# Two attention layers with routed experts on one core: expert outputs added to gathered rows and scattered into the result, with the stages placed anew

## The reference, cut to what matters

```python
# x: 16 batches of 512 tokens, 128 features
h = layernorm(x)
x1 = x + cosformer(h) + dense_experts(h)  # 16 heads of 8; 2 shared experts, 16 routed, top 4
h = layernorm(x1)
p = softmax(h @ router_w + router_b)      # 8 experts
e = argmax(p)                             # each token goes to one
a, g = split(h @ w1[e])                   # w1: 128 x 1024
y = (silu(a) * g) @ w2[e]                 # w2: 512 x 128
out = x1 + causal_attention(h) + max(p) * y
```

## Time and profile before

| what | value |
|---|---|
| runs shown | 1370.4, 1368.79, 1371.34 us; median 1370.4 us |
| profiled execution | 1372.72 us, of which the span from first to last instruction is 1371.5 us |
| PE busy | 1209.3 us, 88% |
| DVE busy | 991.5 us, 72% |
| ACT busy | 912.8 us, 67% |
| POOL busy | 692.6 us, 50% |
| mean granted clock of PE | 0.959 |

### The profile page before, as it was taken

The page is one execution under the profiler, slowest core; times in us unless marked ns, Lnnn a source line. Parts: engine busy times, 40 slices in busy tenths (PEclk is TensorE's granted clock), DMA queues, the critical chain, the costliest instruction groups (busy, mean ns, idle before and its releaser), DMA issues.

```text
span 1371.5 us, 28942 instructions
## 1 busy us (share of the span) xinstructions
PE 1209.3 (88%) x10216; PEld 700.1 (51%) x10216; DVE 991.5 (72%) x2378; ACT 912.8 (67%) x1233; POOL 692.6 (50%) x1093
## 2 busy tenths in 40 slices
PE   2675999999999999999999999999986999899990
PEld 1342445445454545454454545454432476799990
DVE  2163888888888988888888989888868462344545
ACT  1141777778687868777786877787773667577760
POOL 6324455554536464554545464655543345466760
PEclk9898999999999999999999999999996799999995
DMA  7323505050524416060515335060615210111118
GB/s 224 63 57 64 111 19 115 20 103 27 96 53 71 91 32 120 11 115 20 103 34 88 72 52 105 19 120 14 111 37 171 74 29 25 31 48 50 50 48 250
DMA packets 80300, 100.90 MB, mean 74 GB/s; under 512 B 8800, under 2 KB 56672, under 8 KB 79776
## 3 DMA queue, kind: packets, MB, share of 16 engines
q1 hardware_dynamic: 75680, 89.85, 29.9%
q0 software_dynamic: 4480, 9.22, 2.3%
HBM read 73.50 MB, written 25.01 MB: 72 GB/s over the span
## 4 chain that ended last, share of the span: by engine, by line
PE 63%; DVE 20%; issue 5%; ACT 4%; POOL 4%; DMA 3%; ACTq 0%; SPq 0%; DVEq 0%; POOLq 0%
PE PS L628 9%; PE PS L595 8%; PE PS L440 7%; PE PS L484 7%; PE PS L561 5%; PE PS L639 4%; PE PS L580 4%; PE PS L423 4%; DVE xn L824 3%; PE PS L434 2%; DVE nm L985 2%; DMA early<-gate_rows 2%; PE PS L462 2%; PE PS L570 2%; DVE ra L933 1%
## 5 line engine op out<-in xcount | busy, mean ns | idle before, releaser
L735 ACT ACTIVATE flow<-PS 128x1024 f32<-128x1024 f32 x320 | 321.2, 1028 | 129.4 <-PE PS L580 112.1
L1146 POOL TENSOR_SCALAR_AFFINE_SELECT flow<-flow 128x256 f32<-128x256 f32 (+1 forms) x448 | 191.0, 444 | 374.3 <-ACT flow L735 371.7
L595 PE MATMUL PS<-flow 128*32 128x512 f32 (+3 forms) x2048 | 181.2, 455 | 6.2 <-POOL flow L1146 6.2
L985 DVE TENSOR_REDUCE nm<-PS 128x2 f32<-128x1024 f32 x128 | 154.6, 1220 | 42.3 <-PE PS L549 38.9
L1133 POOL TENSOR_TENSOR early<-early 128x512 f32<-128x512 f32 x128 | 160.7, 1270 | 20.9 <-DMA early<-gate_rows 20.0
L484 PE MATMUL PS<-early,down 128*128 128x512 f32 x288 | 151.8, 637 | 18.4 <-POOL early L1133 17.9
L726 ACT COPY qp<-PS 2x1024 f16<-2x1024 f16 x128 | 128.5, 1004 | 51.0 <-PE PS L570 49.8
L440 PE MATMUL PS<-xnT,up 128*128 128x512 f32 x288 | 152.6, 625 | 3.7 <-DVE at L908 3.4
L987 DVE TENSOR_REDUCE nm<-PS 128x2 f32<-128x768 f32 x128 | 121.6, 950 | 32.4 <-PE PS L549 32.3
L628 PE MATMUL PS<-xsT,w1s 128*128 128x128 f32 x1152 | 141.5, 276 | 3.0 <-DVE act L1079 2.9
L1076 DVE SCALAR_TENSOR_TENSOR tanh<-tanh,PS 128x512 f32<-128x512 f32 x72 | 49.5, 687 | 130.0 <-ACT tanh L769 130.0
(11 more groups left out here) (178 smaller groups left out, 2263.3 us busy)
## 6 DMA issues: line engine op xcount, KB each, us to landing
early<-gate_rows SPq DMA_DIRECT2D x32, 1024.0 KB, 10.8
qp<-relay_q SPq DMA_DIRECT2D x64, 128.0 KB
kp<-relay_k SPq DMA_DIRECT2D x64, 128.0 KB
xsb<-xs SPq DMA_DIRECT2D x76, 64.5 KB, 1.8
relay_k<-qkh SPq DMA_DIRECT2D x32, 128.0 KB, 2.3
early<-in_w SPq DMA_DIRECT2D x1, 4096.0 KB, 14.8
out_y<-X SPq DMA_DIRECT2D x4, 1024.0 KB, 7.9
relay_q<-qkh SPq DMA_DIRECT2D x16, 128.0 KB, 2.3
```

What stands on the lines that cost most here:

```text
L595: ins = pe.matmul(m.PS[32 * j:32 * j + 32, m.PV, kt * P:], m.vst[b % 2][:, kt, 4 * g + j, :], m.pt[:, r, k * L + o:k * L + o + L - kt * P] ...
L735: act.activation(m.pt[:, n % RING, :], m.PS[:, i:i + 2, :].rearrange("p k c -> p (k c)"), ACT.Exp, scale=1.0 / SCALE).then_inc(s["exp"], 1)
L985: dve.tensor_reduce(nm[:, 3, 2 * n:2 * n + 2], ps, AX_X, ALU.max, negate=True).then_inc(s["max"], 1)
L1146: ins = pool.affine_select(part, part, [[0, part.shape[1]], [1, P]], ALU.is_ge, nothing, base=0, channel_multiplier=-1)
```

## The change

- The rows sorted to the experts carry two extra columns, the token number and the probability (`expert` writes the maximum into column D + 1 of `xn[1]`; `pmax` is gone). Rows of padding carry the number `NOROW`, which lies outside the result.
- A new stage `keep` stores each batch's x2 to a DRAM buffer once the batch is done (SP). For the last two batches (`LATE`) it stores x1 instead, and `out` overwrites X with the attention's output alone.
- For each tile DVE casts the token column to row numbers (`rows`), POOL gathers those rows of the buffer into `x2g`, DVE computes output x probability + gathered row (`outputs`, from PSUM), and POOL scatters that into the result. Both indirect DMAs have a bounds check that skips rows outside. ACT no longer copies the output.
- The load, the products, the sums and the stores at the end are gone. In their place POOL adds X of the last two batches to the result with two accumulating DMAs.
- U = 6 tiles are in flight. `spares` only clears `x2g`. A load waits also for the sum that reads its column of probabilities.
- All places of FIRST, SECOND and ATTENTION are new.

```diff
-U = 4
+U = 6
...
 FIRST = placed(
-    stats0=[-57.35],
-    norm0=[-49.85],
-    xnT0=[-47.65],
-    kvr=[-46, -45.65, -45.5, -44.4],
-    up=[-43, -40.85, -39.8, -38.8, -38.75, -36.4, -36.15, -35.2, -35],
-    q=[-41.75],
-    kv=[-41.6],
-    route0=[-43.7],
-    gate=[-41.3],
-    attn0=[-40.4],
-    gT=[-40.05],
-    at0T=[-39.05])
+    stats0=[-56.25],
+    norm0=[-53.2],
+    xnT0=[-51.6],
+    kvr=[-50.05, -47.1, -45.9, -45.65],
+    up=[-41.1, -40.55, -40.45, -40.3, -39.25, -38.9, -38.7, -36.05, -35.75],
+    q=[-41.65],
+    kv=[-41.15],
+    route0=[-41.65],
+    gate=[-40.75],
+    attn0=[-40.2],
+    gT=[-40.2],
+    at0T=[-36.6])
 SECOND = placed(
-    down=[-34.9, -33.5, -33.2, -30.9, -30.85, -30.2, -29.3, -28.65, -27.8],
-    gated=[-36.55, -35, -34.1, -33.5, -33.05, -32.45, -29.9, -28.6],
-    x1=[-27.4],
-    stats1=[-26.25],
-    norm1=[-25.65],
-    xnT1=[-25.1],
-    rope=[-24.3, -23.3],
-    parts=[-23.55, -22.35],
-    relay=[-20],
-    v=[-19.2],
-    logits=[-23.65],
-    route1=[-20.45],
-    expert=[-19.65],
-    ranks=[-17.05],
-    sort=[-18.25, -17.5, -14.95, -13.45])
+    down=[-35.7, -32.85, -32.25, -31.05, -31, -30.95, -30.05, -30, -28.65],
+    gated=[-35.85, -35.7, -35, -34.15, -33.9, -33.3, -33.05, -33],
+    x1=[-28.25],
+    stats1=[-28.2],
+    norm1=[-25.9],
+    xnT1=[-25.6],
+    rope=[-23.25, -22.3],
+    parts=[-22.4, -21.15],
+    relay=[-19.9],
+    v=[-13.2],
+    logits=[-24.9],
+    route1=[-24.15],
+    expert=[-19.45],
+    ranks=[-19.1],
+    sort=[-17.55, -17.45, -16.7, -16])
 ATTENTION = placed(
-    score=[0, 0.1, 1.45, 3.05, 7.4, 8.2, 9.25, 10.3, 12.35, 13.05, 13.85, 14.05, 14.6, 14.7, 15.2, 15.35, 15.75,
-           16.1, 16.95, 19.25],
-    max=[-7.8, -7.8, -7.75, -3.6, -2.85, -2.05, 0.4, 0.75, 1.2, 1.35, 3.45, 4.1, 4.85, 4.9, 5.25, 5.9, 7.1, 8.3, 9.3,
-         10.35],
-    mparts=[-2.85, 3.3, 8.15, 10.35],
-    mrows=[-0.85, 5.2, 10.4, 12.1],
-    value=[1.45, 7.5, 9.7, 12.65, 13.95, 14.35, 14.95, 15.65, 17, 19.2, 20.15, 20.2],
-    sums=[14.4, 20.45],
-    heads=[14.85, 21.25],
-    mT=[22.85],
-    out=[24.55])
+    score=[-0.25, 0.55, 0.6, 2.85, 3.7, 6.6, 7.3, 9.25, 10, 11.8, 12.7, 13.85, 14.35, 14.45, 15.65, 16.75, 16.95,
+           17.75, 18.35, 18.35],
+    max=[-6.65, -5.65, -3.6, -3, -2.9, -1.15, -0.95, -0.7, 0.85, 0.9, 1.35, 3.65, 4.35, 4.45, 5.85, 6.05, 7.6, 8.75,
+         8.85, 9.9],
+    mparts=[-2, 3.9, 7.75, 10.15],
+    mrows=[-1, 5.2, 9, 11.7],
+    value=[1.35, 5.3, 5.3, 11.85, 13.1, 14.15, 14.95, 16.45, 17.05, 18.25, 20.15, 20.85],
+    sums=[13.9, 21.1],
+    heads=[20.75, 23.3],
+    mT=[24.85],
+    out=[25.95])
+
+KEEP = placed(
+    keep=[-26.9, 32.85])
...
-LAST += [(tile(n) + 0.05, "load", n + U) for n in range(NTILE)]
+LAST += [(tile(n) + 0.05, "load", n + U) for n in range(NTILE - U)]
...
-    out = [(NS * b + at, name, b, i) for b in range(B) for at, name, i in FIRST + SECOND + ATTENTION]
+    out = [(NS * b + at, name, b, i) for b in range(B) for at, name, i in FIRST + SECOND + ATTENTION + KEEP]
     out += [(NS * (B - 1) + at, name, 0, i) for at, name, i in LAST]
+    out = [stage for stage in out if stage[1] != "keep" or (stage[2] >= B - LATE) == (stage[3] == 0)]
...
-        m.xn = [sb(f"xn{n}", [P, NT, D + n], where=side) for n in range(2)]
+        m.xn = [sb(f"xn{n}", [P, NT, D + 2 * n], where=side) for n in range(2)]
...
-    m.xsb = sb("xsb", [P, U, D + 1])
+    m.xsb = sb("xsb", [P, U, D + 2])
+    m.x2g = sb("x2g", [P, U, D])
...
-    m.xs_d = nc.dram_tensor("xs", [(E1 + 1) * CAP, D + 1], F32, kind="Internal").ap()
-    m.ys_d = nc.dram_tensor("ys", [B * L + (U + NTILE + 2) * P, D], F32, kind="Internal").ap()
+    m.xs_d = nc.dram_tensor("xs", [(E1 + 1) * CAP, D + 2], F32, kind="Internal").ap()
+
+    m.x2_d = nc.dram_tensor("x2", [B * L, D], F32, kind="Internal").ap()
     m.x_d = io["x"].rearrange("b (t p) d -> p b t d", p=P)
+    m.x2_b = m.x2_d.rearrange("(b t p) d -> p b t d", t=NT, p=P)
     m.out_d = io["out"].rearrange("b (t p) d -> p b t d", p=P)
+    m.out_r = io["out"].rearrange("b l d -> (b l) d")
...
+LATE = 2
+
+NOROW = 2 * B * L
...
-    def outputs(_, n):
-        act.wait_ge(s["yo_mm"], n + 1)
-        act.wait_ge(s[f"d_ys{n % U}"], 16 * (n // U + 1))
-        act.copy(m.ysb[:, n % U, :], wk(("outputs", 0, n))[:, 0:D]).then_inc(s["ycopy"], 1)
...
     def expert(b, i):
         dve.wait_ge(s["e1"], b + 1)
+        if b:
+            dve.wait_ge(s["d_sorted"], 16 * NT * b)
         then(shares(m.e1[:, :, :], E1, m.p1[:, :, :]))
         dve.tensor_reduce(m.s1[:, 3, :], m.p1[:, :, :], AX_X, ALU.max)
-        then(dve.tensor_reduce(m.pmax[:, b * NT:(b + 1) * NT], m.p1[:, :, :], AX_X, ALU.max))
+        then(dve.tensor_reduce(m.xn[1][:, :, D + 1], m.p1[:, :, :], AX_X, ALU.max))
...
+        ps = wk(("out", b, i)).rearrange("p (t d) -> p t d", t=NT)
         dve.wait_ge(s["out_mm"], b + 1)
-        dve.tensor_tensor(xt, xt, wk(("out", b, i)).rearrange("p (t d) -> p t d", t=NT), ALU.add).then_inc(s["x2"], 1)
+        if b < B - LATE:
+            dve.tensor_tensor(xt, xt, ps, ALU.add).then_inc(s["x2"], 1)
+        else:
+            dve.wait_ge(s["d_x1"], 16 * (b - (B - LATE) + 1))
+            dve.tensor_copy(xt, ps).then_inc(s["x2"], 1)
...
+    def rows(_, n):
+        u = n % U
+        dve.wait_ge(s[f"d_xs{u}"], 16 * (n // U + 1))
+        if n >= U:
+            dve.wait_ge(s[f"d_ys{u}"], 16 * (n // U))
+        dve.tensor_copy(m.rowu[:, u:u + 1], m.xsb[:, u, D:D + 1]).then_inc(s["rows"], 1)
+
+    def outputs(_, n):
+        u = n % U
+        dve.wait_ge(s["yo_mm"], n + 1)
+        dve.wait_ge(s[f"d_xg{u}"], 16 * (n // U + 1))
+        if n >= U:
+            dve.wait_ge(s[f"d_ys{u}"], 16 * (n // U))
+        dve.scalar_tensor_tensor(out=m.ysb[:, u, :], in0=wk(("outputs", 0, n))[:, 0:D], scalar=m.xsb[:, u, D + 1:D + 2],
+                                 in1=m.x2g[:, u, :], op0=ALU.mult, op1=ALU.add).then_inc(s["ycopy"], 1)
...
-    n = B * NT // Q
-    for q in range(Q):
-        y, xq = m.yg[:, q * n:(q + 1) * n, :], m.X[:, q * n:(q + 1) * n, :]
-        dve.wait_ge(s[f"d_xs{q}"], 16 * (NTILE // U + 2))
-        then(dve.tensor_tensor(y, y, m.pmax[:, q * n:(q + 1) * n].unsqueeze(2).to_broadcast([P, n, D]), ALU.mult))
-        dve.tensor_tensor(xq, xq, y, ALU.add).then_inc(s["final"], 1)
...
-        pool.tensor_scalar(m.spare[:, :], const(m, K_T)[:, 0:1], float(B * L + U * P + 1), None, ALU.add).then_inc(s["spare"], 1)
-        pool.tensor_scalar(m.rowu[:, :], const(m, K_T), float(B * L), None, ALU.add).then_inc(s["spare_rows"], 1)
-        pool.wait_ge(s["spare_rows"], 1)
-        pool.wait_ge(s["spare"], 1)
+        pool.memset(m.x2g[:, :, :], 0.0).then_inc(s["spare"], 1)
+
+    def rows(_, n):
+
+        u = n % U
+        if n == 0:
+            pool.wait_ge(s["spare"], 1)
+            pool.wait_ge(s["d_x2"], 16 * (B - LATE))
+            pool.wait_ge(s["d_x1"], 16 * LATE)
+        if n >= U:
+            pool.wait_ge(s["ycopy"], n - U + 1)
+        pool.wait_ge(s["rows"], n + 1)
         alone()
-        for u in range(U):
-            pool.indirect_dma_start(m.ys_d, bass.IndirectOffsetOnAxis(ap=m.rowu[:, u:u + 1], axis=0),
-                                    m.zeros[:, 0:D], None).then_inc(s[f"d_ys{u}"], 16)
-
-    def rows(_, n):
-        u = n % U
-        pool.wait_ge(s[f"d_xs{u}"], 16 * (n // U + 1))
-        pool.wait_ge(s[f"d_ys{u}"], 16 * (n // U + 1))
-        if n:
-            pool.wait_ge(s["nextspare"], n)
-        pool.tensor_scalar(m.isno[:, :], m.xsb[:, u, D:D + 1], 0.0, m.spare[:, 0:1], ALU.is_lt,
-                           ALU.mult).then_inc(s["spare"], 1)
-        pool.wait_ge(s["spare"], n + 2)
-        pool.tensor_scalar(m.rowu[:, u:u + 1], m.isno[:, :], m.xsb[:, u, D:D + 1], None, ALU.add).then_inc(s["rows"], 1)
-        pool.tensor_scalar(m.spare[:, :], m.spare[:, :], float(P), None, ALU.add).then_inc(s["nextspare"], 1)
+        pool.indirect_dma_start(m.x2g[:, u, :], None, m.x2_d, bass.IndirectOffsetOnAxis(ap=m.rowu[:, u:u + 1], axis=0),
+                                bounds_check=B * L - 1, oob_is_err=False).then_inc(s[f"d_xg{u}"], 16)
 
     def outputs(_, n):
         u = n % U
         pool.wait_ge(s["ycopy"], n + 1)
         pool.wait_ge(s["rows"], n + 1)
         alone()
-        pool.indirect_dma_start(m.ys_d, bass.IndirectOffsetOnAxis(ap=m.rowu[:, u:u + 1], axis=0),
-                                m.ysb[:, u, :], None).then_inc(s[f"d_ys{u}"], 16)
+        pool.indirect_dma_start(m.out_r, bass.IndirectOffsetOnAxis(ap=m.rowu[:, u:u + 1], axis=0), m.ysb[:, u, :], None,
+                                bounds_check=B * L - 1, oob_is_err=False).then_inc(s[f"d_ys{u}"], 16)
...
+    pool.wait_ge(s["x2"], B)
+    for u in range(U):
+        pool.wait_ge(s[f"d_ys{u}"], 16 * (NTILE // U))
+    for b in range(B - LATE, B):
+        pool.dma_start(m.out_d[:, b], m.X[:, b * NT:(b + 1) * NT, :], accum_op=ALU.add).then_inc(s["d_out"], 16)
+    pool.wait_ge(s["d_out"], 16 * LATE)
```

(20 more changed lines are left out.)

28 lines of the change are left out of this document (13 added, 15 removed).

## The result

The changed kernel took 1456.3 us, median of 4 runs (1445.3 to 1464.4), against 1370.3 us before: ratio 1.062, 95% interval 1.054 to 1.071. **It is slower by 86 us**; the forecast was 24 us faster.

A forecast was written before the change was run, and what follows sets the result against it. PE was taken to set the steady and tile pace, with an idle-PE end. Terms -24.5 + 2 + 0 + 4 + 0 - 3 - 2.5 + 0 = -24 us gave 1348.7 us profiled, 1346.5 us named; range 1331 to 1364 us.

The forecast's parts named there:

- Part 5, the steady stage: New order of work in 180 to 980 us: 0, since PE at 96.7% is a cover any order must keep.
- Rival C: Steady batches: waits around mrows and mparts worsen, up to 4.3 us a batch, 1406 us; break-even 1.7 us; chance 0.08.
- Part 3: DVE and ACT in the tiles: DVE's cast may wait 0.97 us for POOL's DMA, needing 2.7 of 2.79 us.
- Part 1, the end: After the last scatter: two accumulating DMAs replace load, sums and stores; tail 8 us for 32.5, -24.5 us.
- Part 2, POOL: Tile stage: POOL's second indirect DMA, the gather, just fits in PE's 2.79 us a tile; +2 us.
- rival A: Tile stage: POOL becomes the bound at 1.21 us per indirect DMA, +12.7 us, 1357 us; chance 0.15.
- Hidden: Tile stage: the gather, issued 5.6 us before its sum needs it, lands in 2.4 us, so costs no wait.
- Part 3, the mixed stage: 22 tiles beside the last attention: PE's bank is freed about 0.7 us later by DVE, +4 us (0 to +15).
- Part 5, filling: First batches: q and the sorts placed earlier save about 2 us each, some lost elsewhere; -3 us (-5 to +2).
- Draining: Last batches: sorts stand further ahead of the tables, removing a 2.50 us wait; -2.5 us (-2.5 to +2).
- Rival D: The end: accumulating DMAs are slow, 12.8 us, giving 1355 us; chance 0.07.
- chance of 0.08 for slower: Whole kernel: the probability given to a slower result, beside 0.89 for faster and 0.03 for same.

The follow-up runs named there:

- e2: The kernel of before with only the new tables of places: 1435.1 us, ratio 1.049.
- e1: The changed kernel with the old places put back: 1362.4 us, ratio 0.996.
- n2: The changed kernel with the old places and without the gather of the old rows: 1359.3 us.
- c3: The changed kernel, unaltered, measured again on chip E, which showed no late starts of ACT: 1416 us.
- e3: The changed kernel without the gather of the old rows and its wait, so outputs lack the residual: 1411.7 us.
- v1b: e1 with ACT again copying the output off its bank in the 21 tiles sharing PE with the last attention, on chip D: 1351.2 us.

## Why the prediction was wrong

- **Part 5, the steady stage, "0"**, is the step that failed. I wrote that a PE at 96.7% is a cover any order must keep. High use says what a wait would cost, not that an order has no wait. The places alone cost 67 us (e2), 51 of them in these batches: PE waits for DVE's norm, which POOL's products hold up, and the clock falls in six of the twelve batches of the changed kernel.
- **Rival C** was the right side with the wrong place. I looked at `mrows` behind `mparts`; that wait fell (13.9 to 3.0 us at PE's mask matmuls). The wait came at `xnT0` behind `norm0`: 37.9 us in 12 times. The gap between them shrank from 2.2 to 1.6 slots (5.5 us of slack before, none after), and the gated products went from eight spread slots (36.55 to 28.6 ahead) to three (35.85 to 33), right across `norm0`. I had the lever in hand in Part 3 (a cast held up by POOL) and used it for the tile cast alone. Rival C also lacked a part of the price: PE's new waits lowered the clock. Of the 51 us in twelve batches (4.3 each, its own upper figure) some 38 are waits and 12 slower matmuls. That 1416 us lies only 10 us above its upper end is luck in part: its waits were at another place, and the slower filling and the slower clock were not in it. Its 1.7 us a batch as the point of break-even was not put to a test.
- **Part 1, the end**: right. Tail 9.2 us for a forecast 8; the accumulating DMAs landed in 5.0 us (forecast 4.0), the two issues took 2.77 us. -23.3 for -24.5.
- **Part 2, POOL, "+2"**: right in kind. The gather took 1.02 us and the gap 0.30, and PE still begins a tile every 2.79 us but for a few, so rival A did not come true. The gather cost 4.2 us (158.4 in e1, 154.2 in n2) or 2.6 (151.4 in c3, 148.8 in e3): the last tile's sum comes 1.7 to 1.9 us later behind its matmuls, the rest are single tiles of up to 3.33 us. "Hidden" was too much: DVE waits for its landing (38.2 us in 44 times on chip E).
- **Part 3, the mixed stage, "+4 (0 to +15)"**: mis-sized. The mechanism was the one described; it measured 11 to 13 us (e1 against v1b), the 14.2 us of waits all but uncovered, against my reading of 78.2 of 87 us busy. The sum for DVE with a cast held up should have read 1.84 + 0.97 = 2.8 us, a little over the tile's 2.79, and not 2.7; it didn't matter, as no cast of the tile stage took more than 0.16 us (c3, e1).
- **Part 5, filling, "-3"**: the second batch's first sum was 2.2 us earlier (125.4 for 127.6), as worked out. By the first x2 it was 14.3 us late: the third batch's first sum came 7.1 us later (125.4 to 195.0 us: the same 378 matmuls, clock 0.85 where it was 0.92), and from there to the first x2 PE worked 45.4 of 47.0 us where before it worked 39.4 of 39.8: the new order puts 6 us more of PE's work ahead of it. **Draining, "-2.5"**: the first table operation waits for no DMA any more, as said, but what that gained can't be read beside the rest.
- **Rival D** did not come true (5.0 us to land, not 12.8). **The chance of 0.08 for slower**: with places changed in every stage and no row that prices an order, it was much too low. The sum of the ending alone, -18.5 us without Part 5, stands against e1's -5.4: the bank was costed at 4 us and took 11 to 13, the gather at 2 and took 4. v1b gained 18.2 us (against its chip's 1369.4), but that number agrees by luck, since v1b avoids the bank's cost, which the sum counts.
